# A decoder layer on one core: the order of two steps in the tensor queue, and the slots at which the vector queue does its side work

## The reference, cut to what matters

```
def step(S, inp):                      # one step of time, for every batch and head
    qt, kt, vt, at, gft = inp
    bs1 = jnp.einsum('bhk,bhkv->bhv', kt, S)
    S1 = S + at[..., :, None] * bs1[..., None, :]
    S2 = jnp.exp(gft)[..., None] * S1
    bs2 = jnp.einsum('bhk,bhkv->bhv', kt, S2)
    S3 = S2 + at[..., :, None] * bs2[..., None, :] + kt[..., :, None] * vt[..., None, :]
    o = jnp.einsum('bhk,bhkv->bhv', qt, S3)
    return (S3, o)
...
out3 = jnp.stack([z, z, o], axis=2).reshape(B, 3 * N, H, HD)
out = out3[:, -N:]                     # only a third of the rows of out carry an o
...
x = _layernorm(x + attention(x))       # LN_1
x = _layernorm(x + cross_attention(x, ctx))   # LN_2
x = _layernorm(x + shared_experts(x) + routed_experts(x))   # LN_3
```

## Time and profile before

| | |
|---|---|
| three timed runs | 2442.62, 2441.83, 2436.6 us; median 2441.83 us |
| the profiled execution | 2442.62 us, its span 2440.8 us |
| DVE busy | 2092.3 us, 86% of the span |
| PE busy | 1754.8 us, 72% |
| POOL busy | 1145.5 us, 47% |
| ACT busy | 663.2 us, 27% |
| chain that ended last | DVE 61%, PE 18%, issue 8%, POOL 7% |

### The profile page before, as it was taken

One profiled execution on the slowest core, in us unless ns is written; L12 is line 12 of the kernel. 1 busy time (PEld: TensorE's weight loads), 2 busy tenths in 40 slices (PEclk: granted clock), 3 DMA queues, 4 the chain that ended last, 5 costly groups with the idle time before them and its releaser, 6 DMA issues.

```text
span 2440.8 us, 31859 instructions
## 1 busy us (share of the span) xinstructions
PE 1754.8 (72%) x9438; PEld 1322.4 (54%) x9438; DVE 2092.3 (86%) x5941; ACT 663.2 (27%) x1457; POOL 1145.5 (47%) x1228
## 2 busy tenths in 40 slices
PE   4258987998699869976898250357887569867993
PEld 2135766676567656765677130244575446754683
DVE  5999999999999999999899999998998989942000
ACT  2132244223422432233222110161222611223221
POOL 2544454565356535553564477353752663213203
PEclk7567998999899989998999665567898669976997
DMA  8000342334233414341345030000344003530243
GB/s 270 22 5 15 126 149 70 119 127 140 76 118 129 149 66 138 131 150 42 106 138 182 25 97 9 20 1 1 101 169 169 18 1 110 203 119 18 102 168 110
DMA packets 175109, 238.51 MB, mean 98 GB/s; under 512 B 28657, under 2 KB 148074, under 8 KB 174954
## 3 DMA queue, kind: packets, MB, share of 16 engines
q1 hardware_dynamic: 140874, 194.46, 23.6%
q10 hardware_dynamic: 27936, 25.44, 3.3%
q0 software_dynamic: 6144, 16.79, 2.1%
HBM read 202.09 MB, written 33.16 MB: 96 GB/s over the span
## 4 chain that ended last, share of the span: by engine, by line
DVE 61%; PE 18%; issue 8%; POOL 7%; ACT 3%; DMA 2%; SPq 0%; POOLq 0%; ACTq 0%; DVEq 0%; another core or an unknown queue 0%; PEldq 0%
DVE ps L1590 13%; DVE ps L1571 11%; DVE prod L1563 9%; DVE terms L1578 8%; DVE terms L1573 5%; PE ps L639 4%; PE ps L630 2%; PE ps L575 2%; PE ps L566 2%; DVE rec_out L1519 2%; PE ps L523 2%; DVE rec_in L1519 2%; DVE stats L1279 1%; PE ps L521 1%; DMA pj<-in_wpT 1%
## 5 line engine op out<-in xcount | busy, mean ns | idle before, releaser
L1590 DVE TENSOR_REDUCE ps<-terms 128x64 f32<-128x320 f32 x1024 | 451.4, 489 | 0.0
L1571 DVE TENSOR_REDUCE ps<-prod 128x16 f32<-128x272 f32 x1024 | 399.9, 438 | 0.0
L1578 DVE TENSOR_TENSOR terms<-ps,rec_out 128x256 f32<-128x256 f32 x1024 | 384.3, 420 | 0.0
L1563 DVE TENSOR_TENSOR prod<-ps,rec_in 128x256 f32<-128x256 f32 x1024 | 383.5, 418 | 0.1
L630 PE MATMUL ps<-xg,fc 128*128 128x128 f32 x2848 | 351.3, 284 | 32.0 <-PE ps L639 13.1
L630 PEld LDWEIGHTS ps<-xg,fc 128*128 128x128 f32 x2848 | 340.6, 198 | 53.6 <-issue 44.0
L639 PE MATMUL ps<-pj,hT 128*128 128x256 f32 x1424 | 345.9, 398 | 33.0 <-ACT hT L915 33.0
L1165 POOL TENSOR_TENSOR oprod<-SE_out,rec_q 128x320 f32<-128x320 f32 x171 | 147.4, 862 | 385.0 <-DVE SE_out L1582 383.0
L639 PEld LDWEIGHTS ps<-pj,hT 128*128 128x128 f32 x1424 | 274.6, 198 | 88.7 <-ACT hT L915 51.3
L566 PE MATMUL ps<-xtf,fc 128*128 128x512 f32 x512 | 247.2, 622 | 5.5 <-ACT vec L795 3.4
L575 PE MATMUL ps<-pj,hT 128*128 128x256 f32 x1024 | 243.2, 389 | 0.0
(11 more groups left out here) (234 smaller groups left out, 2897.0 us busy)
## 6 DMA issues: line engine op xcount, KB each, us to landing
fc<-in_wfcT SPq DMA_DIRECT2D x80, 1024.0 KB
pj<-in_wpT SPq DMA_DIRECT2D x80, 1024.0 KB
xg_rows<-in_rows ACTq DMA_DIRECT2D x105, 128.0 KB, 2.1
out_rows<-y ACTq DMA_DIRECT2D x89, 128.0 KB, 5.7
in_rows<-o_rows SPq DMA_DIRECT2D x2, 2176.0 KB, 17.3
out_rows<-o_rows SPq DMA_DIRECT2D x2, 2176.0 KB, 17.1
xtp<-in_xT SPq DMA_DIRECT2D x32, 128.0 KB
xin<-in_x SPq DMA_DIRECT2D x8, 512.0 KB, 6.9
```

What stands on the lines that cost most here:

```text
L1563: tt(prod[:, c % PLACED, :, cols, 0:HD], SE[:, old, cols, 0:HD].unsqueeze(1).to_broadcast([P, NV, HC, HD]), rec_in[:, c].unsqueeze(2).to_b ...
L1571: red(SE[:, old, cols, HD:EH].rearrange("p v n -> p n v"), prod[:, c % PLACED, :, cols, 0:HD + 1], AX.X, ALU.add).then_inc(step_done, 1)
L1578: tt(terms[:, cols, :, 0:NV], SE[:, old, cols, HD:EH].unsqueeze(2).to_broadcast([P, HC, HD, NV]), rec_out[:, c].unsqueeze(1).to_broadcast( ...
L1590: red(SE[:, new, cols, 0:HD], terms[:, cols, :, 0:NV + 1], AX.X, ALU.add).then_inc(step_done, 1)
```

## The change

Three things are done. First, in TensorE's queue `finish` moves from before expert 9 to before expert 8, directly behind `second`. Second, in the tail GpSimd normalizes tile 6 directly behind its combine, and VectorE takes the statistics for it at the slot of the divisors (36) instead of slot 75. Third, both slot tables change. No arithmetic is added or removed.

```
-                last_experts(f, (start, attend, weigh, second, finish))
+                def second_and_finish():
+                    second()
+                    finish()
+
+                last_experts(f, (start, attend, weigh, second_and_finish, lambda: None))
...
             combine(6)
+            normalize(LN_3, 6, y_out, y_out)
             rsqrt(LN_2, 7)
             for i in range(MOVES):
                 scatter(7, i)
-            normalize(LN_3, 6, y_out, y_out)
...
-                last_stats(t, 6, BOUND_AT["scatter"] + 8)
+                last_stats(t, 6, BOUND_AT["divisors"])
...
-FREE_AT = {1: 1, "caps": 46, "minima": (40, 42, 43, 44), "sums": (48, 48, 49, 50), "divisors": 51, "divided": 55, "resid": 73, 2: 73, "routing": 85, "gather": 82, "scatter": 94, "combine": 101, 3: 110}
-BOUND_AT = {"gated": 3, 0: 3, "x_plus": 10, 1: 11, "minima": (19, 19, 20, 21), "sums": (36, 36, 37, 37), "divisors": 38, "divided": 42, "resid": 47, 2: 47, "routing": 57, "gather": 28, "scatter": 67, "combine": 46, 3: 53}
+FREE_AT = {1: 1, "caps": 46, "minima": (40, 42, 43, 44), "sums": (50, 51, 52, 54), "divisors": 55, "divided": 60, "resid": 71, 2: 71, "routing": 84, "gather": 82, "scatter": 93, "combine": 101, 3: 109}
+BOUND_AT = {"gated": 3, 0: 3, "x_plus": 10, 1: 10, "minima": (18, 18, 19, 20), "sums": (34, 34, 35, 35), "divisors": 36, "divided": 40, "resid": 44, 2: 44, "routing": 54, "gather": 28, "scatter": 63, "combine": 46, 3: 51}
```

## The result

The changed kernel takes 2462.2 us (median of 4 runs, 2461.1 to 2462.5) where the kernel before, on the same chip, takes 2440.9 (2436.6 to 2442.6): a ratio of 1.0089, with a 95% interval of 1.0072 to 1.0107. The forecast was 2461.3. The profiled execution has a span of 2460.7 us, 19.9 more than before. The new lines of the order stand above nearly all others, so that a line of before behind L712 has a number 4 higher here: `resid` is L1298, `divided` L1348, the first of routing L1368, its passes L1405 to L1419.

The account below looks back on a forecast made before the run. VectorE's recurrence was taken to bound the first 2143 us, tile 7's chain the tail. Free periods +13.2, bound periods +2.8 and tail +3.5 made +19.5 us on 2442.62, less 0.8 for the median: 2461.3 us, range 2439 to 2471.

Parts of the forecast that it names:

- Step 1: Periods 2 to 4: `project` starts once the banks are free, behind idle TensorE, at half clock, taking 12.7 us.
- rival 2: `project` keeps the full clock in periods 1 to 4, so waits for it vanish or shrink: 2434.5 us; chance 0.13.
- Step 2: Periods 0 to 4: `resid`, one chunk earlier, waits 27.6 us for `project` instead of 21.1: +6.5 us.
- Step 3: Periods 1 to 4: router's sums late behind two experts, +9.2 us; VectorE's wait at period 4's end goes, -2.5.
- Step 4: Bound periods: waits at L1318 and xin go (-3.4), rsqrt waits +1.4, output products behind `combine` +4.8: +2.8 us.
- Step 5: Tail: statistics of tile 6 delay `divided`, and `project` then takes 12.7 us instead of 11.0: +3.5 us.
- Rival 1: `project` is slow, but the router's sums are in time, so no routing waits in periods 1 to 4: 2452 us; chance 0.22.
- rival 3: The clock rises inside `project`, which then takes 8.7 us: 2440 us; chance 0.10.
- Rival 4: TensorE's lag of some 8 us reaches further waits, 2 us more in each of four periods: 2470 us; chance 0.10.

Follow-up runs that it names:

- after_fill: The changed kernel with 3 to 9 useless products on TensorE ahead of `project` in periods 0 to 4; 2430.4 us, ratio 0.9964.
- order_only: The kernel before with the new order in TensorE's queue alone; 2446.9 us, ratio 1.0064.
- order_fill: The kernel before with the new TensorE order and useless products ahead of `project`, old slots and tail; 2457.9 us, ratio 1.0070.
- fill_gather: The changed kernel with useless products ahead of `project` and GpSimd's gather moved from slot 82 to 88 in the free periods; 2454.0 us, ratio 1.0056.
- after_old_tail: The changed kernel with the two edits of the tail taken back; 2459.0 us, ratio 1.0072.
- tail_only: The kernel before with the two edits of the tail alone; 2441.6 us, ratio 1.0044.
- free_only: The kernel before with the new slot table of the free periods alone; 2452.3 us, ratio 1.0081.

## Why the prediction was right, point by point

**Step 1, the order**: right. `project` runs at half clock for 12.7 us in periods 2 to 4 behind idle stretches of 8.67, 7.85 and 6.19 us, and in period 1 behind 2.87. after_fill shows that this is the cause and not a companion: with the idle stretch filled the same products take 6.8 us, and some 30 us come back. It also comes close to the case of rival 2, in which `project` keeps the full clock: that rival had -13.6 us for the free periods, and in after_fill against before they are 9.6 us shorter (0.6 - 0.5 - 2.1 - 1.1 - 6.5). The waits shrink by 14.1 us, near what the rival had; VectorE's work grows by 4.5.

**Step 2, `resid`**: right in mechanism and size. 4.90, 8.28, 4.91, 4.91 and 5.38 are 28.4 us; 27.6 forecast.

**Step 3, what is late behind**: 10.1 us of routing waits (2.69, 1.57, 2.42, 3.43), 9.2 forecast. The last y came after 17.9 us, not 18.7. The wait of 2.5 us at the end of period 4 is gone as forecast, but not for the reason given, that VectorE comes later: it stays at 2.5 in order_only and order_fill, where VectorE is late at routing as well. It has only moved. A wait of 2.5 (0.4 before) now stands at the statistics of LN_3, for the same late GpSimd, in six of the seven traces with the new slots of the free periods (in fill_gather it is 7.6); in none of the seven with the old slots is it above 0.5. I had put that slot at nothing.

**Not in the prediction at all**: VectorE's work. I took its durations as fixed and priced only waits. They grew by 2.1 to 2.2 us in periods 1 to 3 and shrank by 1 in periods 0 and 4, +4.5 in all. With the 2.1 of LN_3 and 1.7 from the two sums above, that is 8.3 of the 8.6 us between +13.2 forecast for the free periods and +21.8 measured.

**Step 4, the bound periods**: +2.8 forecast, -1.5 measured. The wait behind `combine` came as forecast (4.63 us for 4.8), though VectorE's other waits for these products shrank by 1.1. The waits at L1318 and xin went (3.4), and the four rsqrt waits grew by 1.4 in all, as forecast. Missing were -4.6 at the rows of o and +1.8 of work: the second halves of LN_1 and LN_2 take 2.1 us more in each of periods 6 and 7 (in period 6 the second half of LN_2 takes 3.13 us, beside GpSimd, where it took 2.03), and other operations give a part back.

**Step 5, the tail**: +3.5 forecast; 2.9 by after_old_tail where the tail is long. Where it is short, it is three times that (tail_only: 9.5), since the statistics then hold `divided` for `combine`. Whether GpSimd's earlier normalizing wins anything was not tried apart.

**The sum** was right to a microsecond, and in part by luck: 8.6 too little in the free periods and 1.4 in the lead-in, against 4.3 too much in the bound periods and 5.4 in the tail, which two traces of one kernel do not fix better than to 3.

**The rivals.** Rival 1 is excluded by the routing waits. Rivals 2 and 3 are excluded for this kernel by the clock of 0.50. The rule behind rival 3 (the Trainium skill, "TensorE: Matmul & The Clock Gate", Part 1), that sustained work brings the clock back, is not borne out by `project`: in the changed kernel it works for 12.7 us at a stretch and stays at 0.50 to its end, in periods 0 to 4, 6 and 7. Other work does bring it back: in period 2 the clock is 1.00 from 1.2 us behind the end of `project` on, in expert 8's products. For the idle half of the rule after_fill and order_fill are as good a pair as one could want: the same products at 1.00 with no idle stretch ahead of them, and at 0.50 behind one of 6.77 us. Rival 4 is not borne out: the one further wait, at LN_3, goes with the slots and not with TensorE's lag, since free_only, which has no routing wait, shows it (2.50), and order_only, with the longer lag, does not (0.38).

## What to carry to other kernels

Before moving work on an engine whose clock follows its load, look at what it does right ahead of the piece: an order that starts a step earlier, but behind an idle stretch, can end it later, and cheap products up to the step's start can turn the sign. Split a period into idle time and work of the bounding engine; here the work of a period repeated to 0.3 us, so that even 2 us of meetings with GpSimd could be read. Price each repair in the kernel in which it will stand: `combine` at 43 was worth 4.9 us alone and nearly nothing once `resid` was in time.

## What the runs showed of the hardware

- Small operations of VectorE (0.15 to 0.23 us) took 0.59 to 0.98 beside GpSimd's element-wise work on 256 or 512 columns, and ended with it; a small reduction beside it took its 0.23 as before.
- `project` at half clock never recovered in 12.7 us of its own work. Entered at full clock behind a gap of 0 to 0.9 us it kept it, with one exception: in period 1 of free_only it lost it 2.4 us after its start, behind a gap of 0.61. Behind a gap of 1.62 us (after_fill, period 3) it kept it; behind 2.38 us (after_fill, period 0) it lost it 1.6 us after its start, and in the tail of before, behind 1.74, after 1.9.
- One and the same kernel has a tail of two lengths, some 9 us apart, with a stall of TensorE of 3.65 us in the middle of a run of transposes, while it waits for a copy that ScalarE begins late. Which one is seen went with the chip in all groups, and the cause is open.
